# Per-token maxima over the feed-forward chunks: two strided reduces on VectorE in place of magnitudes and pairwise maxima

## What is computed

```python
def act_quant(x):
    scale = 127.0 / jnp.clip(jnp.max(jnp.abs(x), axis=-1, keepdims=True), 1e-05)
    return jnp.clip(jnp.round(x * scale), -128, 127) / scale

h = bit_linear(x, w1)                                # (4, 512, 1024)
h = depthwise_conv1d(h.transpose(0, 2, 1), conv_w, conv_b)   # three taps along the tokens
h = jax.nn.silu(h.transpose(0, 2, 1))
return bit_linear(h, w2)                             # act_quant(h) times the rounded w2

x = x + tanh(g_xattn) * xattn(layernorm(x), ctx)
x = x + tanh(g_ffn)   * ffn(layernorm(x))
```

## Time and profile before

| | |
|---|---|
| median of three runs | 256.46 us (254.75 to 257.37) |
| span of the profiled execution, first to last instruction | 256.0 us |
| TensorE matmul busy | 202.0 us, 79% |
| VectorE busy | 190.7 us, 74% |
| ScalarE busy | 143.1 us, 56% |
| GpSimd busy | 81.0 us, 32% |
| mean granted TensorE clock | 0.899 |

### The profile page before, as it was taken

The page is one execution under the profiler, slowest core; times in us unless marked ns, Lnnn a source line. Parts: engine busy times, 40 slices in busy tenths (PEclk is TensorE's granted clock), DMA queues, the critical chain, the costliest instruction groups (busy, mean ns, idle before and its releaser), DMA issues. The chain is left out here.

```text
span 256.0 us, 2960 instructions
## 1 busy us (share of the span) xinstructions
PE 202.0 (79%) x940; PEld 117.9 (46%) x940; DVE 190.7 (74%) x344; ACT 143.1 (56%) x205; POOL 81.0 (32%) x74
## 2 busy tenths in 40 slices
PE   8497899988899969699999579999968078530665
PEld 3163457653553646266546353863546045200233
DVE  1635866887436987779889877885973978899884
ACT  2021124212537757994687699475979327797340
POOL 0120432002343672116057703141571302264200
PEclk9979999999959998997999999779997659985699
DMA  6990000000000000000100000002000000200002
GB/s 222 391 351 2 0 4 0 0 0 3 0 0 0 1 0 3 1 0 4 56 26 0 0 0 0 0 0 82 0 0 3 0 1 0 82 1 0 0 0 85
DMA packets 5372, 8.43 MB, mean 33 GB/s; under 512 B 480, under 2 KB 4704, under 8 KB 4976
## 3 DMA queue, kind: packets, MB, share of 16 engines
q1 hardware_dynamic: 4896, 6.38, 7.1%
q10 hardware_dynamic: 464, 1.90, 2.2%
HBM read 6.18 MB, written 2.10 MB: 32 GB/s over the span
## 5 line engine op out<-in xcount | busy, mean ns | idle before, releaser
L1079 POOL TENSOR_TENSOR hid<-hid,right 128x512 f32<-128x512 f32 x32 | 42.3, 1326 | 50.8 <-DVE hid L668 38.3
L668 DVE SCALAR_TENSOR_TENSOR hid<-u,par,hid 128x512 f32<-128x512 f32 x32 | 37.4, 1176 | 0.0
L363 PEld LDWEIGHTS ps_ox<-vbd,probs 128*128 128x128 f32 x256 | 32.2, 200 | 6.9 <-issue 5.8
L363 PE MATMUL ps_ox<-vbd,probs 128*128 128x34 f32 x256 | 31.9, 282 | 1.3 <-DVE o_s L623 1.1
L926 ACT ACTIVATE hid<-u,par 128x512 f32<-128x512 f32 x32 | 23.0, 718 | 17.4 <-DVE u L663 8.6
L1039 POOL TENSOR_TENSOR rstd<-var,minus_half 128x4 f32<-128x4 f32 (+1 forms) x6 | 9.7, 1618 | 50.0 <-DVE minus_mean L639 39.2
L430 PE MATMUL ps_h<-w1q 128*128 128x512 bf16 x48 | 17.6, 508 | 9.5 <-ACT hid L935 8.2
L953 ACT ACTIVATE hid<-hid,round_off 128x1024 f32<-128x1024 f32 x12 | 13.6, 1149 | 19.8 <-DVE hid L714 19.8
L935 ACT ACTIVATE hid<-hid,par 128x512 f32<-128x512 f32 x32 | 22.3, 709 | 3.1 <-POOL hid L1079 3.1
L930 ACT ACTIVATE right<-u,par 128x512 f32<-128x512 f32 x32 | 22.6, 707 | 0.0
L689 DVE TENSOR_TENSOR hmax<-hmax,mag 128x512 f32<-128x512 f32 x24 | 17.5, 730 | 4.3 <-ACT mag L942 2.7
(11 more groups left out here) (121 smaller groups left out, 342.9 us busy)
## 6 DMA issues: line engine op xcount, KB each, us to landing
x_s<-x SPq DMA_DIRECT2D x4, 512.0 KB, 14.3
out<-x_s SPq DMA_DIRECT2D x6, 256.0 KB, 2.1
w2f<-w_t ACTq DMA_DIRECT2D x1, 1024.0 KB, 10.7
w_attn<-attn_w SPq DMA_DIRECT2D x1, 1024.0 KB, 10.9
w1f<-w_t SPq DMA_DIRECT2D x1, 1024.0 KB, 12.9
cT<-ctx_t ACTq DMA_DIRECT2D x1, 512.0 KB, 4.6
out<-x_s SPq DMA_DIRECT2D x4, 128.0 KB, 1.8
row<-rows ACTq DMA_DIRECT2D x1, 256.0 KB, 6.0
```

The source lines that it names most:

```text
L363: last = nc.tensor.matmul(o_ps[:, k, 2 * e:2 * e + 2, :], probs[:, g % 2, e, k * P:(k + 1) * P], vbd[:, 2 * g + e, :], start=True, stop=True)
L668: nc.vector.scalar_tensor_tensor(out=hid[:, f, :], in0=u[:, f % US, 0:N], scalar=par[:, CW + 3 * f:CW + 3 * f + 1], in1=hid[:, f, :], op0= ...
L1079: nc.gpsimd.tensor_tensor(hid[:, f, :], hid[:, f, :], right[:, f % RIGHTS, :], ALU.add).then_inc(conv_ready, 1)
```

## The change

ScalarE's `magnitude`, the buffer `mag` and `shared_chunks` go. `hidden_max(t, half)` is now one VectorE instruction, a `tensor_reduce` with the maximum of absolute values. It reads `hid` through a view with the chunk as the innermost index: for each of the 512 tokens it fetches 4 values (or 5) that lie 2,048 bytes apart, and writes one. The first half covers chunks 0 to 3 and writes into a ninth chunk that `hid` gets, `hid[:, 8, :]`. The second half covers chunks 4 to 7 and that ninth one and writes `hmax`. The first waits for the SiLU of chunk 3, the second for that of chunk 7 and for the first half.

```diff
-        hid = sb("hid", [P, FC, N])
+        hid = sb("hid", [P, FC + 1, N])
         hmax = sb("hmax", [P, N])
-        mag = sb("mag", [P, FC, N])
...
             def transpose_hmax(t):
-                pe.wait_ge(max_step, t.count(FC, FC))
+                pe.wait_ge(max_step, t.count(2, 2))
...
-            def hidden_max(t, f, shared=(), before=0):
-
-                if f in shared:
-                    dve.wait_ge(hid_ready, t.count(FC, f + 1))
-                    nc.vector.scalar_tensor_tensor(out=mag[:, f, :], in0=hid[:, f, :], scalar=-1.0, in1=hid[:, f, :],
-                                                   op0=ALU.mult, op1=ALU.max).then_inc(own_mag_ready, 1)
-                    dve.wait_ge(own_mag_ready, before + shared.index(f) + 1)
-                if f == 0:
-                    return
-                if f == 1 and f in shared:
-                    dve.wait_ge(mag_ready, t.count(FC, 2))
-                elif f not in shared:
-                    dve.wait_ge(mag_ready, t.count(FC, f + 1 + (f + 1 in shared)))
-                if f == 1:
-                    nc.vector.tensor_tensor(hmax[:], mag[:, 0, :], mag[:, 1, :], ALU.max).then_inc(max_step, 2)
-                elif f > 1:
-                    dve.wait_ge(max_step, t.count(FC, f))
-                    nc.vector.tensor_tensor(hmax[:], hmax[:], mag[:, f, :], ALU.max).then_inc(max_step, 1)
+            def hidden_max(t, half):
+
+                dve.wait_ge(hid_ready, t.count(FC, FC // 2 * (half + 1)))
+                if half == 0:
+                    tiles, dst = hid[:, 0:FC // 2, :], hid[:, FC, :]
+                else:
+                    dve.wait_ge(max_step, t.count(2, 1))
+                    tiles, dst = hid[:, FC // 2:FC + 1, :], hmax[:]
+                nc.vector.tensor_reduce(dst, tiles.rearrange("p f n -> p n f"), AX.X, ALU.max,
+                                        apply_absolute_value=True).then_inc(max_step, 1)
...
-                    if feed and not mid and f >= 4:
-                        hidden_max(feed, f - 4, *shared)
+                    if feed and not mid and f == 6:
+                        hidden_max(feed, 0)
...
-                if feed:
-                    for f in range(0 if mid else FC - 4, 1 if mid else FC):
-                        hidden_max(feed, f, *shared)
+                if feed and not mid:
+                    hidden_max(feed, 1)
...
                 if feed and mid:
-                    for f in range(1, 2 if front else 3):
-                        hidden_max(feed, f, *shared)
+                    hidden_max(feed, 0)
                 if mid:
                     residual1(mid)
                     stats2(mid)
...
                 if feed and mid:
-                    for f in range(2 if front else 3, FC):
-                        hidden_max(feed, f, *shared)
+                    hidden_max(feed, 1)
...
-            def magnitude(t, f, shared=()):
-                if f in shared:
-                    return
-                act.wait_ge(hid_ready, t.count(FC, f + 1))
-                nc.scalar.activation(mag[:, f, :], hid[:, f, :], ACT.Abs).then_inc(
-                    mag_ready, 1 + (f + 1 in shared))
```

33 lines of the change are left out of this document (8 added, 25 removed).

## The result

| | before | after |
|---|---|---|
| median of four runs each | 256.08 us (254.75 to 257.37) | 261.14 us (260.75 to 266.41) |
| ratio, 95% interval | | 1.0198 (1.0137 to 1.0259) |
| span of the profiled execution | 256.0 us | 259.7 us |
| VectorE busy | 190.7 us | 199.1 us |
| ScalarE busy | 143.1 us | 130.1 us |

The change makes the kernel 2% slower. The forecast was 250.1 us. Some executions of every kernel here run slower at a lower granted clock: the ratios leave these out, the medians and ranges hold all, and the traces of e6_passes_only, e7_tail_only and e11_pairs_clock are of such executions, so that of these three the stretches are read and not the whole.

The account below looks back on a forecast made before the run. No engine is busy throughout; waits bound the kernel: TensorE's for neg_max, VectorE's maxima, the end chain. Gains 1.4 + 1.4 + 1.8 + 1.75 = 6.35 us off 256.0 give 249.65, median 250.1; range 248.0 to 262.0.

Parts of the forecast that it names:

- the price of a strided read: Both new VectorE reduces: 1.05 ns per value as for contiguous reads, so 2.28 and 2.81 us.
- rival 2: New reduces: strided reads at 1.3 to 1.75 times the contiguous price, giving 253.3 to 261 us; chance 0.12.
- the double: Upper bound for the new reduces' reads: 2.10 ns per value, so 4.4 and 5.5 us.
- Step `(3, 2, none)`: First reduce hidden behind the output projection with 1.35 us to spare, second ending at 204.7 for 206.51; gain 1.8 us.
- Last step: VectorE's own magnitude gone, second reduce ending at 241.05 us for 242.80; gain 1.75 us.
- Passes: Two loop passes: neg_max starts 1.4 us earlier, second reduce ends 1.6 us earlier; 1.4 us gained in each.
- the old wait ahead of `quantise_hidden`: Loop pass, in the working for dearer reads: this VectorE wait absorbs 0.7 us of the second reduce's lateness.
- The exclusion of reduce and GpSimd: Last step: the reduce and GpSimd's add exclude each other, 1.35 us of gain lost, 251.5 us; chance 0.04.
- The loop gains nothing: Loop passes: residual1's 1.2 us delay takes back neg_max's gain, only the last two steps give, 252.9 us; chance 0.06.
- Rival 1: New reduces: strided reads at about double price (1.75 times or more), sum +9.35 us, 265.8 us, slower; chance 0.18.

Follow-up runs that it names:

- e6_passes_only: The change in the two loop passes only, the last two steps as in the kernel before; 263.43 us, ratio 1.0234 to the kernel before.
- e7_tail_only: The change in the last two steps only, the loop passes as in the kernel before; 260.17 us, ratio 1.0158 to the kernel before.
- e11_pairs_clock: e5_pairs with 12 more clock-keeping matmuls ahead of the transposes in step (3, 2, none) and 3 in the last step; 252.85 us, ratio 0.9821.
- e1_probes: Changed kernel plus extra VectorE instructions behind its last work, only their durations counting; reduce of 2,048 values 2.28 us contiguous, 3.62 from four chunks.
- e2_contiguous: Changed kernel with both reduces reading the same number of values contiguously, so hmax holds other maxima; 248.09 us, ratio 0.9711 to the kernel before.
- e4_no_magnitudes: Kernel before without magnitudes, VectorE's seven pairwise maxima reading hid directly; 249.74 us, ratio 0.9785 to the kernel before.
- e5_pairs: Kernel before with maxima mostly by VectorE reduces over two chunks, ScalarE making magnitudes of the last two chunks only; 248.52 us, ratio 0.9655.
- e9_change_again: The whole changed kernel run once more, nothing altered; 263.43 us, ratio 1.0262 to the kernel before.
- e3_clock: Changed kernel with more clock-keeping matmuls ahead of transpose_hmax in the passes and last two steps; 262.78 us, ratio 1.0254 to the kernel before.
- e10_clock_again: The kernel of e3_clock run again, on the same chip as the changed kernel; 261.66 us, ratio 1.0243 to the kernel before.

## Why the prediction was wrong

**The step that failed is the price of a strided read.** It took 1.05 ns per value from the contiguous reduces and argued, from a memset that writes four values 2,056 bytes apart, that steps are free. The reads measured 1.71 to 1.74 ns. The memset row was no evidence for reads, and the trace had no other. The measured 1.6 times lies in rival 2 (1.3 to 1.75 times), which had a chance of 0.12, between the contiguous price and the double that was kept for the range. The result, 261.1, lies within the range only because the range was stretched toward the double price, near its upper end and on the side, slower by more than 1%, that had a chance of 0.22.

The Trainium skill had the sign right. "SBUF — State Buffer", in its section "Specifications (TRN2)", says that each access that crosses to a new 16-byte line pays a penalty, and that the full rate needs at least two hits on a line. e1_probes agrees for four places: free at 8 bytes (2.29 us), dear from 16 bytes on (3.77). The probes do not agree for two places 2,048 bytes apart, where every value crosses and 1.23 us is no more than 1.22, nor for four places 12 bytes apart (1.75 for 1.74), and hardly for three (10%). The measurement decides: the rule as written is too strict there.

**The rest of the sum held, in part by luck.** e2_contiguous is the forecast with its price made true. The prediction had -1.4, -1.4, -1.8 and -1.75 us and 250.1 us; the stretches gave -1.9, -2.2, -1.8 and -1.8, and the median 248.1. `neg_max` starts 0.04 us after its transposes (within 0.1 forecast), `transpose_hmax` starts 1.53 us earlier in the second pass, and e4_no_magnitudes shows the gain without any reduce. But a clock of 1.00 in the passes, which the sum did not count, gave part of their gain: at equal clock about 1.0 us a pass, not 1.4.

**What the price did, place by place**, with 3.70 - 2.28 = 1.42 us more on the first reduce and 4.52 - 2.81 = 1.71 on the second:
- Step `(3, 2, none)`. Forecast -1.8 with the first reduce hidden, with 1.35 us to spare. Timeline of VectorE there, after:

```profile
196.33 3.72 DVE L670 TENSOR_REDUCE hid<-hid 128x512 f32<-128x2048 f32 x1 [4.15 <-ACT hid L913]
199.95 1.28 DVE L621 SCALAR_TENSOR_TENSOR x_s<-ps_b,tg,x_s 128x1024 f32<-128x1024 f32 x1
...
203.50 4.50 DVE L670 TENSOR_REDUCE hmax<-hid 128x512 f32<-128x2560 f32 x1
```

`residual1` (L621) no longer waits for TensorE, so the slack is used up to a tenth, and the second reduce's 1.71 takes the gain: -1.8 + 1.7 = -0.1, measured -0.1.

- Last step. -1.75 + 1.42 + 1.71 = +1.4 at the end of the second reduce. Measured from the step's first `conv_left`: 245.49 - 222.03 = 23.46 us after, 242.80 - 220.55 = 22.25 before, +1.2. Timeline of VectorE, GpSimd and TensorE there, after:

```profile
234.51 3.66 DVE L670 TENSOR_REDUCE hid<-hid 128x512 f32<-128x2048 f32 x1
234.73 1.27 POOL L1040 TENSOR_TENSOR hid<-hid,right 128x512 f32<-128x512 f32 x1 [0.69 <-ACT right L908]
...
241.02 4.47 DVE L670 TENSOR_REDUCE hmax<-hid 128x512 f32<-128x2560 f32 x1 [2.19 <-ACT hid L913]
...
245.55 1.12 PE L425 MATMUL ps_ox<-idf,hmax 128*128 128x128 f32 x4 [5.26 <-DVE hmax L670]
```

The rest up to the stretch's +2.2 comes behind the reduce. The transposes took 1.12 us after a wait of 5.26, where they had taken 0.67, and the scales' transposes took 1.06 (0.65 before).

- Passes. Here a second step failed, that of rivals 1 and 2: they let the reduce's lateness pass through unchanged and then took 0.7 us off for the old wait ahead of `quantise_hidden`. By their working the measured price gives about +0.7 a pass and about 259.3 us in all. The stretches gave +3.1 and +2.3. In the second pass, counted from the last attention maximum, the second reduce ended 1.05 us later than the old maxima (161.47 - 149.21 = 12.26 for 161.02 - 149.81 = 11.21), no more than that working allowed. But `transpose_hmax` stands ahead of `values` of the second group on TensorE. So its wait held both, and both then ran slower: 1.11 - 0.66 = 0.45 and 3.46 - 2.59 = 0.87 us. 1.05 + 0.45 + 0.87 = 2.37 accounts for the +2.3: 1.05 of lateness, which fits the +1.2 at equal clock, and 1.32 of clock, a term that the prediction did not have. And the wait ahead of `quantise_hidden` grew from 0.69 to 1.53 us, instead of absorbing anything:

```profile
167.26 3.48 DVE L696 TENSOR_TENSOR hid<-hid,ps_ox 128x1024 f32<-128x1024 f32 x3 [1.53 <-PE ps_ox L392]
```

**The rivals.** The exclusion of reduce and GpSimd (0.04) is refuted: in the rows of the last step above the reduce takes 3.66 us and the add 1.27 beside it, neither stretched. The Trainium skill's "SBUF — State Buffer", in "Who interferes with whom", has it so, and the trace agrees. "The loop gains nothing" (0.06) is refuted by e2_contiguous and e4_no_magnitudes. Rival 1, at double price or nearly, named the mechanism and the side, but not the size: its 1.75 times were not reached. Its sum of +9.35 us happens to be near the 7.5 of the stretches, since it had the price too high and the wait on TensorE too low.

## What to carry to other kernels

A fp32 operand whose innermost index jumps between four or more places, 16 bytes or more apart, costs about 1.6 times on VectorE and about twice on ScalarE. Arranged in pairs the same work is free on VectorE, and with what e5_pairs moved besides that made the difference between 2% slower and 3.4% faster. Where the whole sum hangs on a pattern that the trace does not show, its price belongs in a probe, or the forecast between its two bounds: a row for writes is not evidence for reads. And where an instruction on TensorE begins to wait, count what stands behind it on its queue, and compare stretches of two kernels at the same granted clock: here it moved a stretch of the same code by up to 2 us.

## What the runs showed of the hardware that I had not expected

- The price has a threshold and then is flat: per reduce of 2,048 values 2.28 us contiguous, 2.29 with steps of 8 bytes, 3.58 to 3.78 with steps of 16 bytes to 2 KB. Steps of 12 bytes are free too (1.75 for 1.74). Two places are free (1.23 for 1.22 us), three cost 10% (1.91 for 1.74), four and eight places 2,048 bytes apart and 64 places 128 bytes apart cost 56 to 59%.
- The tensor_scalar that VectorE ran through four chunks took 2.04 us when the read was strided and 2.03 when the write was, one ns per value, so writes of that pattern are not free there either. Its contiguous form on 2,048 values took 1.23 us in e1_probes (the bitwise and) and, on fp32, 1.22 in the kernel after:

```profile
L735 DVE TENSOR_SCALAR w2f<-w2f 128x2048 f32<-128x2048 f32 x1 | 1.2, 1220 | 0.0
```

- At half clock the same `values` took 3.46 us where it took 1.94 in e2_contiguous at a granted clock of 1.00, and the transposes 1.11 for 0.64. An idle TensorE does not fix when that happens: after 2.06 us in the second pass of the change the transposes took 1.11 us, after 2.39 in that of e9_change_again 0.66, and after 1.76 in the first pass 0.66 in e3_clock and 0.84 in e10_clock_again.
